# Splitting an expert's rows into full tiles of 256 and one or two short tiles in a mixture-of-experts kernel

## What is computed

```python
def _L0_ffn_ref(x, router_w, router_b, gate_w, up_w, down_w):
    logits = jnp.einsum('bth,eh->bte', x, router_w) + router_b
    topv, topi = jax.lax.top_k(logits, TOP_K)
    gates = jax.nn.softmax(topv, axis=-1)
    def body(acc, inputs):
        e, gw, uw, dw = inputs
        w = jnp.sum(gates * (topi == e), axis=-1)
        h = jax.nn.silu(jnp.einsum('bth,fh->btf', x, gw)) * jnp.einsum('bth,fh->btf', x, uw)
        y = jnp.einsum('btf,hf->bth', h, dw)
        return (acc + y * w[..., None], None)
    ...
x = x + _layernorm(_L0_ffn_ref(_layernorm(x, axis=-1), ...), axis=-1)
```

## Time and profile before

| | |
|---|---|
| median of three runs | 1233.63 us |
| lowest and highest | 1232.5 and 1234.02 us |
| the profiled execution | 1234.89 us |
| its span, first to last instruction | 1233.1 us |
| PE busy | 1159.7 us (94%) |
| DVE, ACT, POOL busy | 771.2, 652.6, 554.7 us |
| TensorE's granted clock over the span | 0.98 of 2.4 GHz |
| first transposes of the tile loop | 803.89 us |
| last scatter of the tile loop | 1192.1 us |

### The profile page before, as it was taken

How to read it: one execution, slowest core, us unless ns; L and a number is a source line. 1 busy time by engine, 2 the same in 40 slices (tenths; PEclk the granted TensorE clock), 3 DMA queues, 4 the chain that set the end, 5 groups by cost and what they waited for, 6 DMA issues and landing times.

```text
span 1233.1 us, 29645 instructions
## 1 busy us (share of the span) xinstructions
PE 1159.7 (94%) x9166; PEld 985.2 (80%) x9166; DVE 771.2 (63%) x2380; ACT 652.6 (53%) x1653; POOL 554.7 (45%) x686
## 2 busy tenths in 40 slices
PE   8999999999999999999999999499999999999895
PEld 5878878878788788788788788379999999988762
DVE  5777777886887787777778868523333333333337
ACT  4755656557547557556565573334444444443336
POOL 2244464554654654644645544423333333333326
PEclk9999999999999999999999999689999999999998
DMA  7010110100101100101101001334111111111534
GB/s 280 10 28 14 30 43 9 34 28 24 34 17 30 38 17 26 43 13 30 43 9 34 28 15 43 135 106 116 49 46 51 49 45 51 47 48 43 175 118 189
DMA packets 59676, 67.50 MB, mean 55 GB/s; under 512 B 6896, under 2 KB 49664, under 8 KB 59264
## 3 DMA queue, kind: packets, MB, share of 16 engines
q1 hardware_dynamic: 48720, 41.10, 10.7%
q0 software_dynamic: 8448, 17.45, 4.3%
q10 hardware_dynamic: 2480, 8.61, 2.1%
HBM read 37.98 MB, written 29.15 MB: 54 GB/s over the span
## 4 chain that ended last, share of the span: by engine, by line
PE 65%; DVE 18%; issue 6%; ACT 6%; DMA 3%; DVEq 1%; POOL 0%; ACTq 0%; SPq 0%; POOLq 0%
PE pO L779 9%; PE pO L606 5%; PE pW L639 5%; PE pO L611 5%; PE pA L770 4%; PE pA L771 4%; PE pJ L770 4%; PE pJ L771 4%; PE pJ L561 3%; PE pA L590 3%; DVE qT L1133 3%; DVE ss L1181 3%; PE pJ L519 2%; PE pA L561 2%; PE pJ L639 2%
## 5 line engine op out<-in xcount | busy, mean ns | idle before, releaser
L1656 POOL DMA_INDIRECT expert_out<-y,tail x136 | 130.1, 957 | 263.3 <-ACT y L1038 239.8
L890 ACT ACTIVATE sq<-pO 128x512 f32<-128x512 f32 x128 | 75.8, 592 | 159.3 <-PE pO L606 109.0
L606 PEld LDWEIGHTS pO<-vJ,aT 128*128 128x128 f32 x1024 | 127.9, 192 | 27.0 <-issue 24.0
L606 PE MATMUL pO<-vJ,aT 128*128 128x128 f32 x1024 | 139.1, 279 | 5.5 <-DVE aT L1174 5.5
L1567 POOL DMA_INDIRECT expert_rows<-x1n,rowi x120 | 120.3, 1002 | 47.7 <-issue 29.5
L779 PE MATMUL pO<-wdown_sb,vJ 128*128 128x128 f32 x1088 | 134.1, 277 | 0.0
L1181 DVE TENSOR_REDUCE ss<-sq 128x8 f32<-128x512 f32 x128 | 86.4, 675 | 68.6 <-ACT sq L890 67.6
L779 PEld LDWEIGHTS pO<-wdown_sb,vJ 128*128 128x128 f32 x1088 | 128.4, 194 | 0.0
L1435 DVE TENSOR_TENSOR vJ<-pA,kJ 128x256 f32<-128x256 f32 x136 | 57.6, 425 | 108.3 <-ACT kJ L1027 108.3
L611 PE MATMUL pO<-S_mid,qT 128*128 128x128 f32 x896 | 118.3, 275 | 0.0
L611 PEld LDWEIGHTS pO<-S_mid,qT 128*128 128x128 f32 x896 | 109.1, 192 | 0.0
(11 more groups left out here) (234 smaller groups left out, 2422.5 us busy)
## 6 DMA issues: line engine op xcount, KB each, us to landing
xt<-expert_rows SPq DMA_DIRECT2D x69, 130.0 KB
xa<-x SPq DMA_DIRECT2D x16, 256.0 KB, 3.0
xr<-x SPq DMA_DIRECT2D x16, 256.0 KB, 2.9
after_attention<-x SPq DMA_DIRECT2D x16, 256.0 KB, 2.4
arena<-after_attention ACTq DMA_DIRECT2D x8, 512.0 KB
expert_rows<-zeros SPq DMA_DIRECT2D x8, 390.0 KB
expert_out<-y,tail POOLq DMA_INDIRECT x136
wgate_sb<-wgate SPq DMA_DIRECT2D x1, 2048.0 KB, 9.4
```

The costliest lines, as they stand in the source:

```text
L606: last = mm(o[:, g, h, :, :], aT[:, c % 2, h, g * P:(g + 1) * P], vJ[:, c, h, :], start=(h == 0 and g == 0), stop=(c == 0), skip_group_che ...
L1656: g.indirect_dma_start(out=ys_dram, in_=y[:, k, :], in_offset=None, out_offset=bass.IndirectOffsetOnAxis(ap=tail[:, k, 1:2].bitcast(U32), ...
```

## The change

An expert's rows are divided into full tiles of 256 and then one or two short tiles. With `n` rows the number of full tiles is (n - 1) // 256, at least 1 and for the last expert at least `LAST_FULL` = 2; what is left is 1 to 256 rows. Up to 128 of them are one short tile, more are two. A short tile takes a whole turn of the loop; it starts 128 rows behind the one ahead of it, and of it TensorE multiplies only the first 128 rows: gate and up with 128 columns, and the down products of block 0 only. The load of 256 rows, the two transposes, the silu and the product over 256 columns, both copies to `y` and both scatters stay as they are; the second block of a short tile's `y` holds old values, which go to rows that the next short tile writes or that nobody reads.

```diff
-LAST_LEAST = 3
+LAST_FULL = 2
...
-    TILES = 2 * T // ROWS + E - 1 + LAST_LEAST
+    TILES = 2 * T // ROWS + 2 * E + LAST_FULL - 1
...
-            sp.wait_ge(counts_ready, 1)
-            ends = [sp.value_load(cum_i[0:1, e:e + 1], min_val=e + 1, max_val=TILES) for e in range(E)]
+            sp.wait_ge(counts_ready, 2)
+            ends = [sp.value_load(cum_i[0:1, e:e + 1], min_val=2 * e + 2, max_val=TILES) for e in range(E)]
+            fulls = [sp.value_load(full_i[0:1, e:e + 1], min_val=2 * e + 1, max_val=TILES) for e in range(E)]
...
             for e in range(E):
-                with sp.Fori(0 if e == 0 else ends[e - 1], ends[e]) as t:
-                    load_tile(e, t)
+                first = 0 if e == 0 else ends[e - 1]
+                with sp.Fori(first, fulls[e]) as t:
+                    load_tile(t, (t - first) * ROWS + e * CAP, e)
+                with sp.Fori(fulls[e], ends[e]) as t:
+                    load_tile(t, (fulls[e] - first) * ROWS + (t - fulls[e]) * P + e * CAP, e)
...
-            pe.wait_ge(counts_ready, 1)
+            pe.wait_ge(counts_ready, 2)
...
+            fulls = [pe.value_load(full_i[0:1, e:e + 1], min_val=2 * e + 1, max_val=TILES) for e in range(E)]
             rows_transposed(0)
+
+            def expert_tile(e, t, parts):
+                n = parts * P
+                pe.wait_ge(xt_ready, t + 1)
+                for f in range(FB):
+
+                    pe.wait_ge(h_ready, FIRST + t * FB)
+                    mm(bank[f][:, 0:n], wgate_sb[:, e, f * P:(f + 1) * P], xtT[:, 0:n], start=True, stop=True)
+                    mm(bank[f][:, ROWS:ROWS + n], wup_sb[:, e, f * P:(f + 1) * P], xtT[:, 0:n],
+                       start=True, stop=True).then_inc(up_psum, 1)
+                rows_transposed(t + 1)
+
+                pe.wait_ge(y_ready, FIRST + t * 2)
+                for f in range(FB):
+                    pe.wait_ge(h_ready, FIRST + t * FB + f + 1)
+                    for k in range(parts):
+                        last = mm(ybank[k], hT[:, f, k * P:(k + 1) * P], wdown_sb[:, e, f, :],
+                                  start=(f == 0), stop=(f == FB - 1))
+                last.then_inc(y_psum, 1)
...
+                with pe.Fori(0 if e == 0 else ends[e - 1], fulls[e]) as t:
+                    expert_tile(e, t, 2)
+                with pe.Fori(fulls[e], ends[e]) as t:
+                    expert_tile(e, t, 1)
...
-            tile(lower)
-            for u in range(1, LAST_LEAST):
-                tile(lower + u, lambda u=u: lower_rows(u - 1))
-            with act.Fori(lower + LAST_LEAST, total) as t:
+
+            def first_lower_rows():
+                act.wait_ge(y_free, FIRST + lower)
+                lower_rows(0)
+
+            tile(lower, first_lower_rows)
+            tile(lower + 1, lambda: lower_rows(1))
+            with act.Fori(lower + 2, total) as t:
                 tile(t)
```

More of the change, by code:

```diff
@@ L461, in load_tile @@
                 settle(sp)
-                if e == 0:
-                    load_rows(t * ROWS)
-                else:
-                    load_rows(nc.s_assert_within(
-                        (t - ends[e - 1]) * ROWS + e * CAP, min_val=e * CAP, max_val=(e + 1) * CAP - ROWS,
-                        skip_runtime_bounds_check_because="tile t of expert e lies in its own rows"))
-            for e in range(E):
-                with sp.Fori(0 if e == 0 else ends[e - 1], ends[e]) as t:
-                    load_tile(e, t)
+                load_rows(nc.s_assert_within(
+                    row, min_val=e * CAP, max_val=(e + 1) * CAP - ROWS,
+                    skip_runtime_bounds_check_because="tile t of expert e lies in its own rows"))
+            for e in range(E):
+                first = 0 if e == 0 else ends[e - 1]
[3 more added lines that the diff above has]
+                    load_tile(t, (fulls[e] - first) * ROWS + (t - fulls[e]) * P + e * CAP, e)
             total = ends[E - 1]
```

42 lines of the change are left out of this document (18 added, 24 removed).

## The result

| | before | changed |
|---|---|---|
| median | 1233.83 us | 1261.84 us |
| lowest and highest | 1232.5 and 1237.11 us | 1261.46 and 1262.51 us |
| span of the profiled execution | 1233.1 us | 1260.7 us |
| first to last copy of `tail` | 812.67 to 1189.04, 376.37 us | 816.54 to 1215.19, 398.65 us |

The changed kernel is slower: 1.0214 of the time before, 95% interval 1.0195 to 1.0232. The forecast was 1250.6 us with a range up to 1258. The direction and the 71 tiles came as forecast, the size did not: 28 us instead of 17, and 1261.84 lies above the range.

What follows compares the result with a forecast made beforehand. The prediction took TensorE (5.46 us a tile) as the bound, only 0.13 us above the `y` turn (5.33). Loop +12.2, way in +3.3 and lower-row reads +1.5 sum to +17.0 us on 1233.63: 1250.6 us, range 1245 to 1258.

Steps and rivals of the forecast that it cites:

- what bounds the loop: Tile loop: the turn of the single `y` takes 5.33 us, TensorE's 5.46; 71 tiles instead of 68 cost +12.2 us.
- The rival with TensorE's pace: Tile loop: TensorE alone sets the pace, so short tiles take 2.9 us, loop -11.8 us, total 1226.6 us; chance 3%.
- another split: Tile counts: no expert's rest is over 128 rows, so 68 tiles remain, loop -4.2 us, total 1234.2 us; chance 3%.
- the lead is kept: Tile loop: `xt` comes earlier, TensorE's lead is never used up, loop +8.0 us, total 1246.4 us; chance 9%.
- the way in: Ahead of the loop: longer count chain and 16 register loads instead of 8 on SyncE and TensorE, +3.3 us (2.3 to 4.5).
- the late scatters: Tile loop: result scatters that came late before the change were left as they are, with no added time.
- the added loops: SyncE and TensorE: 16 loops for 8 cost a branch each, taken as 0, at most 8 x 0.1 us.
- the reads of the lower rows: Last expert's first tile: four issues on ScalarE wait for `y_free` ahead of `y`, +1.5 us (0 to 3).
- the second batch: Later reads of the lower experts' rows: one tile earlier without a new wait, no price put on them.
- the collision with `xt`: Last expert's tiles: wide reads collide with the load of `xt` both before and after the change, no price put on it.
- the turns at 5.33: Tile loop: 32 tiles, short ones and full ones behind them, go at 5.33 us, the other 39 at 5.46 us.
- The rival's 1258.9 us: Clock falls to half behind pairs of short tiles, slowing the next full tile's gates three times, +8.3 us; chance 12%.

## Where the prediction held, and where it failed

**Right: what bounds the loop.** That the turn of `y` sets the pace and a short tile costs a whole turn is shown from four sides: full width changes nothing, half the work in all tiles changes nothing, 68 tiles instead of 71 take away most of the loss, and with a second `y` the 71 tiles take no longer than the kernel before. The rival with TensorE's pace is out; so are "another split" (142 scatters) and "the lead is kept".

**Right: the way in.** +3.3 forecast, 3.69 in the profile, 3.5 by the run with the chain and loads alone. SyncE's last load stands at 804.8, forecast 803.9: half of that is the later start of the chain.

**Too small, first: the late scatters (4.5 us of the 11 missed).** The step that failed is the sentence that the late scatters of before "are left as they are in both". One is a collision that the change itself makes: a tile in which TensorE is early issues its wide read before the second scatter is through. That could have been read in the trace of before, where the read comes 0.05 us behind the end of the scatter's issue: a TensorE that is early by more turns the order round. The other three are fetches of instructions that meet a scatter. The kernel with two loop bodies and 68 full-width tiles has three such turns, of 7.1 to 7.4 us, where before has one. The Trainium skill ("Runtime: NRT & Kernel Launch", section "Instruction fetch mechanics") says that instructions come in blocks of 16 KiB by DMA and that a taken branch to code that isn't loaded forces a fetch; the trace agrees in size (0.26 MB for 16 packets) and in part in place: the three lie in TensorE's first tile of the fourth and of the sixth expert and in the short tile of the seventh, but the late one of before lies in the second tile of the seventh. Which engine's instructions are fetched the trace does not say. The prediction weighed the added loops by their branches and not by their code. That the fetch delays the scatter is read from the packets: in all late turns of this kind the scatter's last part starts as the fetch ends, and a fetch that meets no scatter makes none. No run took the fetches away, so whether a fetch meets a scatter's transfer is luck of the place, and so is this term's size.

**Too small, second: the reads of the lower rows (+1.5 forecast with bounds 0 to 3; 4.2 in the profile, 2.8 on the kernel before, 2.5 by taking it back).** The 1.9 us at `y` were right. The step that failed is what the prediction says of the second batch and of the collision with `xt`, that they "exist in both, and I put no price on them": the next tile's rows are requested 0.86 us behind the first of the reads (1150.51 and 1151.37 in the kernel before with the reads moved) and TensorE idles about 3 us for them, in the changed kernel (3.29) and in the kernel before with the reads moved (2.88). Two more costs came with it: the second scatter of that turn lands 1.3 us late (3.69 instead of 2.40), and the clock falls to half in the two turns behind (up to 2.6 us).

**Too small, third: the turns at 5.33 (1.9 us).** 32 were forecast and 29 waits for `tail` came, but the late turns are among these 29. The turns below 5.46 gained 3.2 us, against 0.9 before; the forecast counted a gain of 4.2 and nothing for before, whose few it had read itself.

**Not foreseen: behind the loop (1.5 us).** TensorE idles longer ahead of the other half, and its sums start at half the clock.

**The clock inside the loop.** The rival had three gates of 3.46 us more. After the pairs of short tiles the clock fell twice, and each time it cost 0.5 to 0.6 us, since TensorE was ahead of `y`:

```profile
1002.39 0.60 PE L758 MATMUL pT<-cst,xt 128*128 128x128 f32 x2 [2.19 <-DMA xt<-expert_rows]
...
1002.78 1.92 PE L785 MATMUL pO<-wdown_sb,vJ 128*128 128x128 f32 x8
```

So behind the pairs the sign of that rival was right and its price was not: the turn of `y` hides most of it. Where it was not looked for, in the two turns with the reads of the lower rows (1180.89 and 1189.98 above), the clock fell too, and there `y` waited for the down products, so that it cost up to 2.6 us. The rival's 1258.9 us lies nearer to the measured time than the forecast, but by luck, since its three gates cost nothing like 8.3 us.

4.5 + 2.7 + 1.9 + 1.5 + 0.4 (way in) + 0.5 (ahead of the chain) - 0.4 - 0.3 make 10.8 us; the profiled execution took 1262.5 us where the sum had 1251.9, which is 10.6, and 0.2 is rounding.

## What to carry to other kernels

Before taking work from the busiest engine, look for a ring beside it: one buffer that is written, sent and waited for is a clock of its own, and here it stood 0.13 us below TensorE. Work that is cut then comes back as idle time, and each extra turn costs in full. With a second buffer for the result the cut in five tiles was worth something (0.3%), and the whole split with its three extra turns still was not. And an engine that becomes early also issues its transfers early: ask which scatter or load each of them now gets ahead of.

## What the runs showed of the hardware

- A fetch of instructions is a single packet of 16 KB that takes 0.9 to 1.4 us (up to 2.3 us in the kernel with TensorE's work halved). Where it meets the transfers of a scatter, the scatter's last part starts only as the fetch ends (954.74 and 954.76). With one `y` such turns were 1.1 to 2.1 us late, with two `y` none was (1089.85 in the kernel before with two `y`: held up there too, and the turn is 5.46 us). Other fetches made no late turn (939.81 us in before, 895.84 in the changed kernel). The Trainium skill ("Runtime: NRT & Kernel Launch", section "Instruction fetch mechanics") speaks of the engine that waits for its code; here the one that waits is a scatter of GpSimd.
- A wide read of 512 KB that is issued 0.2 to 0.5 us ahead of the end of an indirect scatter's issue held that scatter up by 1 to 3 us (the seven turns of 6.4 to 8.6 us with TensorE's work halved); issued 0.04 us behind it, it did not. In the first turn of every kernel with one `y` and all rows multiplied the read is issued 0.01 to 0.02 us behind it, and that turn is 6.35 us; whether for this reason is open.
- The 57th tile's second scatter comes 3.09 us behind the end of the first, not 0.30, in both kernels and in those of the experiments; with two `y` the turn is 5.46 us all the same. In the changed kernel:

```profile
1131.95 0.96 POOL L1678 DMA_INDIRECT expert_out<-y,tail  x1 [3.09 <-issue]
```

  It comes after the same number of scatters wherever the loop begins, so it seems to be something of GpSimd's own queue; what it is stays open.
- With TensorE's work halved the granted clock was at 0.85 of full over the loop, and the turns of `y` stayed at 5.33 us. Where TensorE was the one waited for, a stretch at half clock cost its full price (6.99 us against 8.43 for the same turn).
